# New order tables for the five queues of a four-layer graph network on one core

## The reference, cut to what matters

```python
x = L0(x, adj)   # pros = softmax(where(adj==0, MASK, q k^T)); 4 times: z = 0.9 * pros @ z + 0.1 * v
x = L1(x, adj)   # softmax(where(adj==0, -inf, Q K^T)) @ V @ Wo
x = L2(x, adj)   # 8 heads, masked softmax, @ V @ Wo
x = L3(adj, adj, x)
#   agg = einsum('dbmn,bnh->bmdh', mask/(sum(mask)+eps), hid); out = relu(agg @ Wd)
#   r, z = sigmoid(...); n = tanh(... + r * ...); out = (1 - z) * n + z * hid; layer norm
```

## Time and profile before

| | |
|---|---|
| median of 3 runs | 1607.36 us (1606.68 to 1610.14) |
| span of the profiled execution | 1605.4 us |
| PE busy | 1547.1 us, 96% |
| DVE busy | 1282.8 us, 80% |
| ACT busy | 1237.9 us, 77% |
| POOL busy | 697.0 us, 43% |
| mean granted clock of TensorE | 0.993 |

### The profile page before, as it was taken

The page is one execution under the profiler, slowest core; times in us unless marked ns, Lnnn a source line. Parts: engine busy times, 40 slices in busy tenths (PEclk is TensorE's granted clock), DMA queues, the critical chain, the costliest instruction groups (busy, mean ns, idle before and its releaser), DMA issues.

```text
span 1605.4 us, 44598 instructions
## 1 busy us (share of the span) xinstructions
PE 1547.1 (96%) x17360; PEld 1405.8 (88%) x17360; DVE 1282.8 (80%) x3164; ACT 1237.9 (77%) x4074; POOL 697.0 (43%) x710
## 2 busy tenths in 40 slices
PE   7888999999999999999999999999999999999986
PEld 6777999899899989998998999899899999998875
DVE  3676888888888888888888888888888888888764
ACT  4677887787888788888878788887878888787652
POOL 1344444434454444445444444544444444444411
PEclk7999999999999999999999999999999999999999
DMA  5100000111110011011001101100110110000000
GB/s 201 34 25 28 28 28 15 34 35 29 34 35 28 15 35 34 28 35 35 27 15 35 35 28 35 34 28 15 35 35 28 35 35 27 15 28 25 18 8 13
DMA packets 71425, 51.64 MB, mean 32 GB/s; under 512 B 4400, under 2 KB 69936, under 8 KB 70576
## 3 DMA queue, kind: packets, MB, share of 16 engines
q1 hardware_dynamic: 71216, 48.79, 10.0%
HBM read 40.39 MB, written 8.39 MB: 30 GB/s over the span
## 4 chain that ended last, share of the span: by engine, by line
PE 67%; ACT 28%; DVE 2%; issue 1%; DMA 1%; POOL 0%; SPq 0%; POOLq 0%; DVEq 0%; ACTq 0%
ACT E L706 9%; PE bank_A L400 7%; ACT E L770 7%; PE bank_B L400 7%; PE bank_B L629 6%; PE bank_A L444 6%; PE bank_C L400 5%; PE bank_B L444 4%; PE bank_A L629 3%; PE bank_A L418 3%; PE bank_B L412 3%; ACT PT L712 2%; PE bank_A L430 2%; PE bank_X L550 2%; PE bank_A L528 2%; PE bank_B L438 2%
## 5 line engine op out<-in xcount | busy, mean ns | idle before, releaser
L850 POOL TENSOR_TENSOR E<-E,rsum 128x512 f32<-128x512 f32 x256 | 270.7, 1058 | 472.5 <-DVE rsum L1041 317.6
L858 POOL TENSOR_TENSOR rstd<-var,minus_half 128x2 f32<-128x2 f32 x128 | 93.7, 741 | 407.9 <-DVE var L995 407.9
L712 ACT ACTIVATE PT<-bank_C 128x512 f32<-128x512 f32 x128 | 85.8, 670 | 59.9 <-PE bank_C L438 59.9
L1002 DVE TENSOR_SCALAR y<-y,mv,rstd 128x256 f32<-128x256 f32 x192 | 93.0, 527 | 25.8 <-POOL rstd L858 25.8
L943 DVE COPY_PREDICATED_SCALAR bank_A<-absent,fill 128x512 f32 x128 | 92.3, 742 | 15.2 <-PE bank_B L430 14.4
L400 PE MATMUL bank_A<-xT_hi,w_hi 128*128 128x256 f32 x384 | 99.7, 284 | 0.0
L400 PE MATMUL bank_A<-xT_hi,w_lo 128*128 128x256 f32 x384 | 97.1, 277 | 0.0
L943 DVE COPY_PREDICATED_SCALAR bank_B<-absent,fill 128x512 f32 x128 | 94.7, 740 | 0.0
L770 ACT ACTIVATE E<-bank_A,nmax 128x128 f32<-128x128 f32 x256 | 92.4, 402 | 2.5 <-DVE nmax L1037 2.5
L706 ACT ACTIVATE E<-bank_B,nmax 128x128 f32<-128x128 f32 x256 | 94.2, 435 | 0.0
L706 ACT ACTIVATE E<-bank_A,nmax 128x128 f32<-128x128 f32 x256 | 90.8, 382 | 4.1 <-DVE nmax L946 4.1
(11 more groups left out here) (225 smaller groups left out, 6299.3 us busy)
## 6 DMA issues: line engine op xcount, KB each, us to landing
xt_in<-in_xt SPq DMA_DIRECT2D x64, 128.0 KB, 2.3
absent<-in_adj SPq DMA_DIRECT2D x64, 128.0 KB, 2.7
x_in<-in_x SPq DMA_DIRECT2D x32, 256.0 KB, 3.0
out<-y SPq DMA_DIRECT2D x32, 256.0 KB, 2.2
adj<-in_adj SPq DMA_DIRECT2D x32, 128.0 KB, 3.3
adjT<-in_adjt SPq DMA_DIRECT2D x32, 128.0 KB, 3.1
stage<-in_weights SPq DMA_DIRECT2D x3, 1024.0 KB, 11.3
row<-in_rows SPq DMA_DIRECT2D x1, 1024.0 KB, 7.9
```

What stands on the lines that cost most here:

```text
L712: nc.scalar.activation(PT0[:, part].rearrange("p g c n -> p (g c n)"), C0[:, :], ACT.Copy, scale=1.0 - ALPHA).then_inc(pt0_ready.sem, 1)
L850: nc.gpsimd.tensor_tensor(e, e, rs[:, part].unsqueeze(2).to_broadcast([P, SB, P]), ALU.mult).then_inc(e_sig.sem, 1)
L858: nc.gpsimd.tensor_tensor(rstd[part][:], var[part][:], minus_half[:], ALU.pow)\
L1002: a = nc.vector.tensor_scalar(y[part][:, g, :], src[g], mv[part][:, g, 0:1], rstd[part][:, g:g + 1], ALU.subtract, ALU.mult)
```

## The change

The lists are replaced. No step, wait, buffer or instruction is added or taken out. Many differences between the old and the new lists are only another place to cut the cycle. This is the diff:

```diff
 ORDER = {
     "tensor": [
-        "n3@4 k0 wo2.0@3 wo2.1@3 hop0.6@1 hop0.7@1 n2@2 back0.6@1 back0.7@1 q0 lab.0@4 lab.1@4 k2@2 q2@2 v2@2 agg.0@4",
-        "n1@1 agg.1@4 s02.0 lab.2@4 lab.3@4 g1@1 v0 agg.2@4 vo1@1 agg.3@4 p0.0 s02.1 s1@1 p0.1 l1w out@4 nh@4 rh@4",
-        "ri@4 ni@4 p0.2 p1@1 z@4 p2.0@2 p0.3 o1@1 hop0.0 hop0.1 cnt@3 back0.0 back0.1 mixt@4 hop0.2 hop0.3 p2.1@2",
-        "p2.2@2 back0.2 back0.3 p2.3@2 hop0.4 hop0.5 hop2.0@2 hop2.1@2 back0.4 back0.5",
+        "n3@4 back0.4@1 back0.5@1 k0 wo2.0@3 hop0.6@1 hop0.7@1 n2@2 back0.6@1 back0.7@1 wo2.1@3 q0 lab.0@4 lab.1@4",
+        "k2@2 q2@2 v2@2 agg.0@4 agg.1@4 n1@1 s02.0 lab.2@4 lab.3@4 g1@1 v0 agg.2@4 vo1@1 agg.3@4 p0.0 s02.1 s1@1",
+        "out@4 p0.1 nh@4 l1w rh@4 ri@4 ni@4 p0.2 p1@1 z@4 p0.3 o1@1 hop0.0 hop0.1 p2.0@2 back0.0 cnt@3 back0.1 mixt@4",
+        "hop0.2 hop0.3 p2.1@2 back0.2 p2.2@2 back0.3 p2.3@2 hop0.4 hop0.5 hop2.0@2 hop2.1@2",
     ],
     "scalar": [
-        "split.1 split.2 t2@3 lab.0@5 q0@1 k2@3 lab.1@5 q2@3 acc.0@5 wtb@4 hi1@2 split.6@3 t1@2 split.4@2 lab.2@5",
-        "exp2.0@3 exp0.0@1 g1@2 lab.3@5 exp2.1@3 exp0.1@1 acc.1@5 p0.0@1 vo1@2 p0.1@1 out@5 nh@5 exp0.2@1 exp1@2 r@5",
-        "exp0.3@1 exp2.2@3 p0.2@1 p1@2 n@5 z@5 p0.3@1 x0 hop0.0@1 hop0.1@1 exp2.3@3 p2.0@3 hop0.2@1 hop0.3@1 p2.1@3",
-        "p2.2@3 p2.3@3 l1w@1 hop0.4@1 hop0.5@1 hop2.0@3 hop2.1@3 split.5@2 hi3@4 k0 t3@4 hop0.6@1 hop0.7@1 split.3@1",
-        "hi2@2",
+        "hop0.3@2 p2.1@4 p2.2@4 p2.3@4 x0@1 hop0.4@2 hop0.5@2 split.5@3 hop2.0@4 hop2.1@4 hi3@5 split.3@2 t3@5 k0@1",
+        "hop0.6@2 hop0.7@2 split.4@2 hi2@3 t2@3 split.2@1 split.6@3 lab.0@5 k2@3 lab.1@5 q2@3 q0@1 acc.0@5 wtb@4",
+        "hi1@2 t1@2 exp2.0@3 lab.2@5 exp0.0@1 lab.3@5 g1@2 exp2.1@3 exp0.1@1 acc.1@5 split.1 vo1@2 p0.0@1 out@5",
+        "p0.1@1 nh@5 exp0.2@1 exp1@2 r@5 exp0.3@1 p0.2@1 p1@2 exp2.2@3 n@5 p0.3@1 z@5 hop0.0@1 hop0.1@1 exp2.3@3",
+        "p2.0@3 l1w@1 hop0.2@1",
     ],
     "gpsimd": [
-        "sh.3@6 sc.1@3 sc.0@2 e2.0@3 e0.0@1 sh.0@2 ne1@2 e0.1@1 sh.1@3 e2.1@3 e0.2@1 e1@2 e0.3@1 e2.2@3 e2.3@3",
-        "pow.3@5 absent.0 absent.2@2 pow.1@2 pow.0@1 pow.2@3 sc.3@5",
+        "e2.0@3 e2.1@3 e2.2@3 absent.0 e2.3@3 absent.2@2 pow.3@5 ne1@1 pow.1@2 pow.0@1 sc.0@1 sc.3@5 sh.3@5 e0.0",
+        "pow.2@3 e0.1 sc.1@2 sh.0@1 sh.1@2 e0.2 e1@1 e0.3",
     ],
     "vector": [
-        "v0@1 acc.3@5 rec0.1@1 acc.4@5 rec2.1@3 acc.5@5 fill0.2@1 max0.2@1 fill1@2 o_hi@5 o_lo@5 fill0.3@1 max1@2",
-        "max0.3@1 rec0.2@1 fill2.2@3 rec1@2 max2.2@3 fill2.3@3 gate@5 rec0.3@1 sum@5 rec2.2@3 split.5@3 nrm.2@4",
-        "max2.3@3 mixa@5 mixb@5 mixc@5 back0.0@1 back0.1@1 x0 split.1 cols@0 rec2.3@3 y1@2 bn.3@5 agg.3@5 back0.2@1",
-        "eps.3@5 back0.3@1 bn.1@2 guard@4 nrm.3@5 split.6@3 hop2.0@3 rcnt@4 agg.1@2 l1w@1 eps.1@2 hop2.1@3 back0.4@1",
-        "y2.0@3 back0.5@1 nrm.1@2 lo3@4 y2.1@3 split.4@2 bn.2@3 mask@3 xv@1 lo2@2 agg.2@3 y0.0@1 y0.1@1 bn.0@1",
-        "eps.2@3 agg.0@1 xlo.0@4 eps.0@1 nrm.0@1 xlo.1@4 v2@2 acc.0@4 acc.1@4 acc.2@4 split.3@1 split.2 fill2.0@2",
-        "fill0.0 max2.0@2 lo1@1 max0.0 fill2.1@2 rows@1 xlo.2@4 max2.1@2 rec2.0@2 fill0.1 max0.1 rec0.0 xlo.3@4",
+        "acc.1@5 acc.2@5 fill2.0@3 max2.0@3 fill0.0@1 lo1@2 max0.0@1 fill2.1@3 max2.1@3 xlo.2@5 fill0.1@1 max0.1@1",
+        "rec0.0@1 rec2.0@3 xlo.3@5 rec2.1@3 v0@1 eps.2@4 acc.3@5 rec0.1@1 acc.4@5 acc.5@5 fill0.2@1 max0.2@1 fill1@2",
+        "o_hi@5 o_lo@5 fill0.3@1 max1@2 max0.3@1 rec0.2@1 fill2.2@3 rec1@2 fill2.3@3 max2.2@3 split.1 gate@5 rec0.3@1",
+        "max2.3@3 split.3@2 split.4@2 sum@5 nrm.2@4 mixa@5 rec2.2@3 mixb@5 mixc@5 back0.0@1 back0.1@1 rec2.3@3 y1@2",
+        "bn.3@5 agg.3@5 eps.3@5 guard@4 back0.2@1 back0.3@1 bn.1@2 nrm.3@5 x0 agg.1@2 eps.1@2 rcnt@4 l1w@1 hop2.0@3",
+        "hop2.1@3 back0.4@1 back0.5@1 nrm.1@2 cols rows@1 split.5@2 y2.0@3 xv@1 lo3@4 y2.1@3 y0.0@1 lo2@2 bn.2@3",
+        "y0.1@1 bn.0@1 split.2 agg.0@1 eps.0@1 agg.2@3 split.6@2 xlo.0@4 mask@3 nrm.0@1 xlo.1@4 v2@2 acc.0@4",
     ],
     "sync": [
-        "ldw.0 ldw.1@4 ld_adj.2@3 ld_x@2 ld_adj.0@1 ld_adj.1@2 ld_adj.3@4 ld_xt store@6",
+        "ldw.0 ldw.1@2 ld_adj.1@2 ld_x@2 store@7 ld_adj.3@3 ld_adj.0 ld_xt ld_adj.2@2",
     ],
 }
```

## The result

The changed kernel takes 1643.87 us (median, 1642.63 to 1645.56); the kernel before, on the same chip, 1608.57 us (1606.68 to 1610.14). The ratio is 1.0219, 95% interval 1.0203 to 1.0236: slower by 2.2%, outside the range of the forecast.

A forecast was written before the change was run, and what follows sets the result against it. It took PE, busy 96% of the span, as the bound. Span 1605.4 + 12.9 (full periods) - 3.0 (ends) = 1615.3 us, with 1.96 us from span to median 1617.3 us; range 1609 to 1625.

The forecast's parts named there:

- the collision at the end of L3: POOL's `e2` products beside DVE's `nrm.2`, `mixa`, `mixb`, `mixc`: 0.49 us gain lost and 0.46 us more a period.
- The step on `mixc`: On DVE, `mixc` waits for POOL's `e2.2` after `mixb`, so `mixt` starts at 41.5, not 40.55; period 47.4 us.
- one more turn: Rival: `z` late, `e2.2` and `absent.0` both go ahead of `mixc`; +39.5 us in full periods, 1644 us; chance 0.11.
- The three waits on PE: PE waits at `s02.1` (0.19 us), `s1` (0.23) and `back0.1` (0.07); new order ends them, 0.49 us a period.
- Order works: Rival: POOL and DVE don't hurt each other between `mixb` and `mixc`; period 46.5 us, time 1590.7 us; chance 0.32.
- The ends: Fill and drain outside the full periods: +1.1 us and -2.6 us in the first periods, -1.5 us in the drain.

The follow-up runs named there:

- e2: Not a run: the operations `e2.0` to `e2.3` in POOL's list, code names; no time of their own as a kernel.
- e0: Not a run: the operations `e0.0` to `e0.3` in POOL's list, code names; no time of their own as a kernel.
- the run with both moves: Changed kernel with `sc.1`, `sh.0`, `sh.1` ahead of `e0.0` in POOL's list and `rec2.2` behind `mixc` in DVE's: 1594.25 us, ratio 0.9917.
- the first collision taken away: Changed kernel with only `sc.1`, `sh.0`, `sh.1` two to four places earlier in POOL's list: 1609.77 us, ratio 1.0009.

## Why the prediction was wrong

The direction was right and the size was not: 1617.3 us forecast, 1643.87 measured, +0.46 us a period forecast, +1.41 measured.

**The step that failed** is this one: "`o_lo` meets `sh.0` and `sh.1` on POOL (offset 29 to 30) and may lose 0.5 us, of which `ri` needs none: it comes two projections later." The collision was seen and put at nothing. It costs 1.07 us a period, 28 x 1.07 = 30.0 us, more than the whole miss of 26.6 us. The miss in the period, 1.41 less 0.46 = 0.95 us, adds up so, to within 0.01: 1.07 for `o_lo`, 0.11 for both collisions together, 0.12 that the period without either collision is longer than forecast (46.59 for 46.47), and 0.36 the other way, because the collision at the end of L3 costs 0.59 and not the 0.95 in the sum. Two things are wrong in the step. `o_hi`, one step earlier, is a copy inside SBUF, and such a copy is shut out too: `o_hi` waits for `sh.0` (0.43 to 1.15 us, 0.72 more), then `o_lo` for `sh.1` (0.69 to 1.67, 0.98 more), 1.70 us in sum. And the slack of `ri` was not worked out: the sum was 1.70 us of delay against some 0.9 us of slack, as 0.79 us came out at `ri` (its distance from `rh` 2.15 us, and 1.36 with `sc.1`, `sh.0` and `sh.1` moved). The run with both moves shows the slack directly: `o_lo` ends at offset 30.35 (920.92 less 890.57), and `ri` starts at 31.30. Behind the wait the next groups are longer too, in the run with `rec2.2` later against the run with both moves: `ri` by 0.12, `p0.2` by 0.08, `p1` by 0.05; with the 0.79 that is 1.04 of the 1.07.

**The mechanism was right.** DVE and POOL shut each other out and take turns. The Trainium skill, page "SBUF — State Buffer", section "Who interferes with whom", says that copies and casts can enter a two-port mode, and that VectorE then contends with GpSimd: by that rule `o_hi` belonged in the sum, and the trace agrees (1.15 us beside `sh.0`, 0.43 without).

**The step on `mixc` was right with `ri` in time, and not in the changed kernel.** The prediction had `mixb`, `e2.2`, `mixc` in turn and a period of 47.4. With only the first collision taken away the rows show just that, `mixc` recorded at 1.41 and a period of 47.18; its cost is 0.59 us and not the 0.95 that the sum took (0.46 and the 0.49 of lost gain). In the changed kernel `z` was 1.03 us later by `ri` and other delays, and `e2.2` won the turn before `mixb`. `z` had been placed too early even without them: ready at 39.0 by the prediction, at 39.43 with the first collision taken away, at 40.46 in the changed kernel. PE waited at L665 for L1113, as said, but `mixc` was not the stretched one.

**The rival "one more turn"** gave 1644 us and a period of 48.4, and both came out. Its mechanism didn't. It had `absent.0` hold up `mixc`; the row of `mixc` shows 0.77 us over `absent.0`, 0.08 more than alone. Its condition, a late `z`, did hold. That the number fits is chance: over half of the loss is at `o_lo`, which this rival doesn't have.

**The three waits on PE** were right. `p0.0` to `s02.1` takes 0.56 us, `s02.1` to `s1` 1.10 us, the wait of L550 on ACT is gone and that of L430 on `exp` down from 11.6 us to 4.7, and without the two collisions the period is 46.59 (46.47 forecast). So 0.37 of the 0.49 us were there to be had. "Order works", 1590.7 us, is what the new lists give with four steps moved: 1594.25.

**The ends.** -3.0 us forecast, -7.7 + 3.7 = -4.0 measured; the sum is right and its terms aren't. The start won 7.7 us, where +1.1 and -2.6 stood. The drain lost 3.7 us, where -1.5 stood. In the second stretch of the drain PE waits 1.8 us for `xlo` (L1072) and 1.5 us for `y` (L1052, or its normalization L1002 by the weight loads' waits). Both waits are there in the run with both moves (1.8 and 1.7), so the two collisions don't make them. The drain is 142.4 us there and 140.4 in the kernel before with POOL's new list (one trace each), so POOL's list alone doesn't make the 3.7 us either; which of the others does was not separated.

## What to carry to other kernels

Two engines that exclude each other are one resource for the instructions that need it: when a list moves one of them by some microseconds, set all of its operations against all of the other engine's, with their kinds of operands, and not only at the place that one is looking at. For each overlap work out the delay in full (also of copies) and then the slack of the first reader in microseconds; "it comes later" is no slack. The price of leaving it out was 2.2% here, and moving four steps turned it into a gain of 0.8%.

## What the runs showed of the hardware

Which DVE instructions are shut out depends on where their operands are. In the changed kernel, beside a POOL operation with two SBUF inputs (L850, L875), medians: `mixb` (two SBUF inputs) 1531 ns for 692, `o_lo` 1662 for 691, `nrm.x` (one SBUF input to SBUF) 1126 for 409, `o_hi` 1133 for 428. DVE instructions that read PSUM aren't touched, not even with a second input in SBUF: L1085 484 ns beside L850 and 484 alone, L1102 675 for 692, L1037 654 for 691.

Not expected: `absent.x`, a POOL operation with one int32 input and output in SBUF (L839), doesn't shut DVE out once it runs. 27 times `mixc` ran beside it in 766 ns for 691; in the kernel before with POOL's new list 27 times `mixb` in 693 for 693. It gets longer itself, 1.30 us for 0.85, where a DVE instruction with two SBUF inputs had begun before it. That doesn't fit the rule that the prediction took over, by which any GpSimd instruction that reads SBUF holds the pair. Why it waits and doesn't make others wait stays open; no run here took it apart.
